# PSUM as seven single banks, maxima and exponentials in halves, and a layer schedule with its own start for each part of a visit

## The reference

```python
out = jnp.einsum('nec,ecd->nd', cb, exp_out)      # each token: the gated answers of its two experts
...
for i in range(NL):                                # NL = 6 layers
    q, k = _rope(q.reshape(B, L, H, HD)), _rope(k.reshape(B, L, H, HD))
    x = x + _attn(q, k, v, src_mask).reshape(B, L, D) @ so_w[i].T
    ...                                            # cross-attention, then the feed-forward part
```

## Time and profile before

| What | Value |
| --- | --- |
| median of 3 runs | 2237.33 us (2235.38 to 2241.73) |
| the profiled execution | 2237.12 us |
| its span, first to last instruction | 2235.3 us |
| mean granted TensorE clock | 0.905 of 2.4 GHz |
| busy, share of the span | PE 80%, PEld 34%, DVE 74%, ACT 66%, POOL 46% |
| instructions | 36409 |
| HBM traffic | 82.15 MB read, 67.85 MB written |

### The profile page before, as it was taken

The page is one execution under the profiler, slowest core; times in us unless marked ns, Lnnn a source line. Parts: engine busy times, 40 slices in busy tenths (PEclk is TensorE's granted clock), DMA queues, the critical chain, the costliest instruction groups (busy, mean ns, idle before and its releaser), DMA issues.

```text
span 2235.3 us, 36409 instructions
## 1 busy us (share of the span) xinstructions
PE 1791.6 (80%) x13134; PEld 765.2 (34%) x13138; DVE 1653.7 (74%) x3177; ACT 1476.8 (66%) x1840; POOL 1021.2 (46%) x1498
## 2 busy tenths in 40 slices
PE   3564184158899999999999999999999999998561
PEld 2332173012233333333333333333333333333331
DVE  7766111367788888888888888888888888877675
ACT  2443021026688788888888888888888888878452
POOL 2443703422345545455645445544544554534531
PEclk9766597569899999999999999999999999999765
DMA  3001121222443343334343235333244334331100
GB/s 100 1 0 38 56 85 52 67 67 37 92 96 85 66 88 79 79 87 92 83 97 78 54 84 108 95 72 87 53 103 95 82 69 94 81 78 41 30 11 10
DMA packets 153714, 154.87 MB, mean 69 GB/s; under 512 B 32247, under 2 KB 137523, under 8 KB 153523
## 3 DMA queue, kind: packets, MB, share of 16 engines
q1 hardware_dynamic: 151487, 148.34, 28.7%
q0 software_dynamic: 2048, 4.20, 0.7%
HBM read 82.15 MB, written 67.85 MB: 67 GB/s over the span
## 4 chain that ended last, share of the span: by engine, by line
PE 39%; DVE 11%; DMA 9%; ACT 7%; POOL 7%; issue 6%; SPq 2%; DVEq 0%; POOLq 0%; ACTq 0%
PE ps L1323 9%; DMA q<-scratch_queries 9%; PE ps L1287 5%; PE ps L1436 5%; PE ps L1276 4%; DVE smax L1819 4%; ACT big L1549 4%; POOL hat L126 3%; PE ps L1427 3%; PE ps L1335 2%; PE ps L1400 2%; PE ps L1310 2%; PE ps L1298 1%; DVE maxima L1826 1%; PE ps L1376 1%
## 5 line engine op out<-in xcount | busy, mean ns | idle before, releaser
L1549 ACT ACTIVATE big<-ps 128x1024 f32<-128x1024 f32 x960 | 951.9, 1023 | 241.4 <-PE ps L1287 222.3
L1819 DVE TENSOR_REDUCE smax<-ps 128x2 f32<-128x1024 f32 x768 | 921.5, 1219 | 204.4 <-PE ps L1276 181.2
L1323 PE MATMUL ps<-big,vaug 128*32 128x512 f32 x3072 | 419.8, 617 | 0.0
L1276 PE MATMUL ps<-k,q 49*128 49x512 bf16 x1536 | 298.1, 391 | 68.3 <-DMA q<-scratch_queries 51.5
L1287 PE MATMUL ps<-q,k 52*128 52x512 bf16 x1536 | 300.6, 390 | 16.1 <-DVE smax L1819 8.3
L1826 DVE TENSOR_REDUCE maxima<-ps 128x8 f32<-128x616 f32 x192 | 150.1, 795 | 42.8 <-PE ps L1310 40.5
L1276 PEld LDWEIGHTS ps<-k,q 49*128 49x128 bf16 x1536 | 72.8, 94 | 297.6 <-ACT big L1549 99.3
L1718 POOL TENSOR_SCALAR var_next<-mv_next 128x4 f32<-128x4 f32 x24 | 5.6, 233 | 356.1 <-DVE mv_next L1886 356.1
L1287 PEld LDWEIGHTS ps<-q,k 52*128 52x128 bf16 x1536 | 75.7, 94 | 187.2 <-DVE smax L1819 63.9
L1736 POOL TENSOR_TENSOR rot<-rot,cs 128x512 f32<-128x512 f32 x72 | 91.9, 1277 | 101.0 <-DVE rot L1837 101.0
L1436 PE MATMUL ps<-w,hT 128*128 128x128 f32 x768 | 112.4, 292 | 4.2 <-ACT hT L1622 4.2
(11 more groups left out here) (308 smaller groups left out, 2934.5 us busy)
## 6 DMA issues: line engine op xcount, KB each, us to landing
k<-scratch_keys SPq DMA_DIRECT2D x48, 384.0 KB
q<-scratch_queries SPq DMA_DIRECT2D x48, 384.0 KB, 8.1
cq<-scratch_cross_queries SPq DMA_DIRECT2D x48, 384.0 KB, 5.8
scratch_keys<-rparts SPq DMA_DIRECT2D x24, 384.0 KB, 2.5
scratch_queries<-rparts SPq DMA_DIRECT2D x24, 384.0 KB, 2.4
scratch_cross_queries<-rparts SPq DMA_DIRECT2D x24, 384.0 KB
scratch_keys<-rparts SPq DMA_DIRECT2D x24, 256.0 KB, 2.2
scratch_queries<-rparts SPq DMA_DIRECT2D x24, 256.0 KB, 2.7
```

The costliest lines, as they stand in the source:

```text
L1276: last = nc.tensor.matmul(out[:, u], m.q6[rows, v % 2, 2 * g + pr, qt * P:(qt + 1) * P], m.k6[rows, v % 2, 2 * g + pr, :], start=True, sto ...
L1323: last = nc.tensor.matmul(m.ps[32 * j:32 * j + 32, pv_bank, :], of_head(m.vaug, v % 2 * TB + kt, g, j), of_quad("self", q)[:, j, :], start ...
L1549: nc.scalar.activation(of_quad(kind, p // 2)[:, p % 2 * 2:p % 2 * 2 + 2, :], banks("exp" if kind == "self" else "cross exp", p), ACT.Exp, ...
L1819: nc.vector.tensor_reduce(m.smax[:, n % 2, qt, :, pr], banks("max", i), AX.X, ALU.max).then_inc(s_read["self"], 1)
```

## The change

- **Banks.** Banks 0 to 6 are seven single banks for all uses; the weighed values collect in bank 7. `shared` hands them out one at a time; a pair of scores takes two of them, wherever they lie. `bank_freed` names each use's reader. `free_pair` waits for both banks before the first of the two matmuls. `take_aux` goes.
- **Halves.** A maximum, a cross maximum, an exponential and the copies of turned rows in the closing block become two instructions, one per bank, each with an increment of its semaphore (the copies with one for both). Counts that wait for them double.
- **Fetch.** The 32 gathers and the combination move from `mixture` into `layers`, batch by batch. `begin_layers` goes: a batch's statistics run on VectorE, its root on POOL and its normalisation on VectorE, and each batch's first statistics wait for `begun`. `m.fetch` moves to the part of `big` that the third and fourth buffer of exponentials use, whose first uses wait for `begun`.
- **Places.** All tables are new. A call's place is its offset plus the start of its part in that visit, `STARTS`, with six parts per visit (`PARTS`) and 24 starts per part, instead of one period.
- The rows for the closing block's second half count on a semaphore of their own, and its bias waits for the first half's rows.

On POOL the places give the order: fetch 0, fetch 1, root 0, fetch 2, normalisation of visit 0, fetch 3, rotations of visit 0, root 1, the rest of visit 0's splitting, root 2, normalisation of visit 1, root 3, rotations of visit 1. On VectorE: combine 0, state 0, combine 1, statistics of visit 0, one rotation, combine 2, the other rotation, combine 3, state 1, statistics of visit 1, states 2 and 3, rotations of visit 1, then the first maximum. On TensorE the values of visit 0 and the turn and products of visit 1 stand before the first scores of visit 0.

```diff
@@ mixture, POOL @@
-            for u in range(2):
-                pool.wait_ge(stored[u], 16 * (EXPERTS // 2))
-            for t in range(T):
-                for k in range(TOP_K):
-                    nc.gpsimd.indirect_dma_start(m.fetch[:, k, t, :], None, a["answers"],
-                                                 bass.IndirectOffsetOnAxis(ap=m.fetch_from[:, k, t:t + 1], axis=0)).then_inc(fetched[t // TB], 16)
...
@@ Places @@
-    def put(self, name, count, first, offsets, period):
-        self.of[name] = {i: period * (i // len(offsets)) + offsets[i % len(offsets)] for i in range(first, count)}
+    def put(self, name, count, first, offsets, starts):
+        self.of[name] = {i: starts[i // len(offsets)] + offsets[i % len(offsets)] for i in range(first, count)}
...
@@ layers @@
-    pv_bank, aux = 6, 7
+    banks, pv_bank = 7, 7
...
+    def each(kind, taken, given, count, parts=2, every=1):
+        return [(at(taken, every * i), at(given, i) + u / 8, (kind, i, u)) for i in range(count) for u in range(parts)]
+    uses = each("exp", "PE exp", "ACT exp", VISITS * PER_VISIT) + each("max", "PE max", "DVE max", VISITS * PER_VISIT)
...
+    place, bank_before = shared(uses, banks)
...
+            def free_bank(kind, i, u=0):
+                if bank_before[kind, i, u] is not None:
+                    before, n, half = bank_before[kind, i, u]
+                    freed, per = bank_freed[before]
+                    pe.wait_ge(freed, n + 1 if per == 1 else 2 * n + half + 1)
+                return bank(kind, i, u)
+            def free_pair(kind, i):
+                return [free_bank(kind, i, u) for u in range(2)]
...
@@ max_scores, TensorE (shifted_scores and cross_scores alike) @@
-                out = free_banks("max", i)
+                out = free_pair("max", i)
...
@@ exponentials, ScalarE @@
-                nc.scalar.activation(of_quad(kind, p // 2)[:, p % 2 * 2:p % 2 * 2 + 2, :], banks("exp" if kind == "self" else "cross exp", p),
-                                     ACT.Exp, scale=scale).then_inc(probs[kind], 1)
+                if p % 2 == 0 and before is None and quad[kind, p // 2] >= 2:
+                    act.wait_ge(begun, B // 2 * (quad[kind, p // 2] - 1))
+                for u in range(2):
+                    nc.scalar.activation(of_quad(kind, p // 2)[:, p % 2 * 2 + u, :], bank("exp" if kind == "self" else "cross exp", p, u),
+                                         ACT.Exp, scale=scale).then_inc(probs[kind], 1)
...
@@ POOL @@
+            def fetch_answers(b):
+                for u in range(2 if b == 0 else 0):
+                    pool.wait_ge(stored[u], 16 * (EXPERTS // 2))
+                for t in range(TB):
+                    for k in range(TOP_K):
+                        nc.gpsimd.indirect_dma_start(m.fetch[:, b, k, t, :], None, a["answers"], bass.IndirectOffsetOnAxis(
+                            ap=m.fetch_from[:, k, b * TB + t:b * TB + t + 1], axis=0)).then_inc(fetched[b], 16)
...
@@ row_maxima, VectorE (cross_row_maxima alike) @@
-                nc.vector.tensor_reduce(m.smax[:, n % 2, qt, :, pr], banks("max", i), AX.X, ALU.max).then_inc(s_read["self"], 1)
+                for u in range(2):
+                    nc.vector.tensor_reduce(m.smax[:, n % 2, qt, u, pr:pr + 1], bank("max", i, u), AX.X, ALU.max).then_inc(s_read["self"], 1)
...
@@ VectorE @@
+            def combine(b):
+                dve.wait_ge(fetched[b], 16 * TOP_K * TB)
...
+                for t in range(b * TB, (b + 1) * TB):
+                    last = nc.vector.bn_stats(m.st.bn[:, t, :], m.x[:, t, :])
+                c_chain.link(last)
+                for t in range(b * TB, (b + 1) * TB):
+                    last = nc.vector.bn_aggr(m.st.mv[:, t, :], m.st.bn[:, t, :])
+                last.then_inc(begin_moments, 1)
+            def first_state(b):
+                dve.wait_ge(begin_root, b + 1)
+                for t in range(b * TB, (b + 1) * TB):
+                    last = normalise(nc.vector, m.state[:], m.x[:], t, m.st)
+                last.then_inc(begun, 1)
```

601 lines of the change are left out of this document (328 added, 273 removed), and 12 rows, old and new, of the table OFFSETS.

## The result

The changed kernel takes **2221.04 us** (median of 5 runs, 2213.04 to 2225.59) against 2237.33: 0.992 of the time before, interval [0.9892, 0.9947]. It is faster by 16 us where 70 were forecast, and inside the range.

The account below looks back on a forecast made before the run. TensorE was the near bound, busy 63.4 of 66.35 us per visit, trading banks with VectorE and ScalarE. 2237.1 - 21.8 (fetch) - 10 (placing) - 38 (banks) = 2167 us, range 2112 to 2228.

Parts of the forecast that it names:

- The step that failed: Steady visits: TensorE's wait for the load of the queries, 1.0 us per visit, was taken as unchanged.
- Banks: Steady visits: seven single banks remove half of 3.8 us of waits, 1.9 us per visit, 38 us over 20 periods.
- Halves: Split readers in each visit: VectorE +2.4 us to 58.8, ScalarE +4.0 us to 59.7, both under TensorE's 63.4.
- Waits in TensorE's queue: 72 more waits per visit, two per pair of scores, costed at 0 because running matmuls cover them; 3.7 us uncovered.
- Head and ramp: Before the steady visits: fetch inside the layers gains 21.8 us, parts placed one by one in visits 1 to 3 gain 10.
- Tail: Last visit and closing block: split copies cost about 1 us, new order unpriced; taken as 0, between -8 and +8 us.
- A: Steady visits: slower readers replace banks as what TensorE waits for; period stays 66.35 us, total 2205 us; chance 0.22.
- B: Steady visits: all waits for banks go, 76 us, total 2129 us; chance 0.10.
- C: Steady visits: halves don't overlap, ScalarE reaches 65.7 us, period 68.6, total 2250 us, slower; chance 0.11.
- D: Whole kernel: the head's gain and the halves' cost cancel, total about 2237 us; chance 0.07.
- my list of what would show the forecast wrong: ScalarE halves 0.57 us apart, period 66 us or more, first scores after 445, or tail over 8 us longer.
- the weight loads' waits for the two readers: Steady visits: score weight loads' waits for exponentials and maxima were to fall well under 78 and 63 us.

Follow-up runs that it names:

- run 5: Changed kernel with the keys' preparation put ahead of the queries' on ScalarE, POOL and SP, TensorE's and VectorE's orders kept; 2147.79 us, 0.9603.
- run 15: Changed kernel with the loads of keys and queries each cut into two halves of four head pairs, mask rows at their old place; 2140.31 us, 0.9542.
- run 7: Kernel before the change, with key and query loads cut into two halves and mask rows loaded early; 2201.68 us, 0.9834.
- run 4: Changed kernel with key and query loads cut into two halves and mask rows loaded early; 2144.09 us, 0.9562.
- run 8: Changed kernel with halved loads and early mask rows, but a pair's banks given back only after both halves are read; 2243.84 us, 1.0023.
- run 1: Kernel before the change, with only maxima, cross maxima and exponentials split into two instructions each; 2263.57 us, 1.0101.
- run 11: Changed kernel with all four batches' gathers, combinations, roots and states put first again; 2233.41 us, 0.9973.
- run 12: Changed kernel with the preparation of visits 0 to 3 placed at the later visits' distance from the maxima; 2258.72 us, 1.0082.
- run 2: Changed kernel with the two mask-row loads moved from ahead of the queries' load to after the first keys' store; 2221.61 us, 0.9913.
- run 3: Changed kernel with the two mask-row loads cut into four at the same place ahead of the queries' load; 2215.83 us, 0.9896.

## Why the prediction was wrong

**The step that failed** is the sentence "Another 1.0 us per visit is the load of the queries ..., which the change leaves". It became 2.6 us, and brought the falls of the clock with it. The change had new places for every call, and I followed them through POOL's queue in the head, but not through the preparation of a steady visit, where the keys' last part had moved behind a split of maxima on POOL and behind three stores on SP. That made 14.7 us into 18.3; with the keys first on all three queues it is 15.6 and the wait is all but gone (run 5). I had also taken the wait as a fixed cost of a transfer, while it is what is left of a chain after TensorE's work beside it. The trace of before had a sign of this, in its chain of waits over the whole span, by lines (share of the span):

```profile
PE ps L1323 9%; DMA q<-scratch_queries 9%; PE ps L1287 5%; PE ps L1436 5%; PE ps L1276 4%; DVE smax L1819 4%; ACT big L1549 4%; POOL hat L126 3%; PE ps L1427 3%; PE ps L1335 2%; PE ps L1400 2%; PE ps L1310 2%; PE ps L1298 1%; DVE maxima L1826 1%; PE ps L1376 1%
```

The landing of this load is the second of all lines there; in run 15 it is not among the first fifteen.

The steady period by its parts, before to after: wait for queries +1.5, other idle time of TensorE -1.1, busy time +0.6, in which 2.15 us more per visit ran at 1.2 GHz; together +1.07. 64.45 was forecast, with 1.0 of the wait still in it. Without the wait (run 15) the period is 63.95, so the other terms of the visits came to 0.5 us less gain than forecast.

**Banks**, -1.9 us per visit: near in size, 1.4 to 1.7 (run 7 against 15 and 4), but not for the reason given, so that the size was luck. I let half of the waits go; really the early release of a half, which I had as one point among three, carries 4.4 us per visit (run 8), and the rest of the change in the visits costs 2.7 (run 8 against 7).

**Halves**: VectorE +2.4 us per visit forecast, +2.2 measured; ScalarE +4.0, and +2.2 measured in run 1. ScalarE's exponentials start 0.50 us apart or less, not 0.52. By the table in the Trainium skill (VectorE: DVE Perf Modes, section on the TRN2 errata) they would have cost 5.0 and 5.7, as an estimate; both measured costs are less than half of it. What stands beside the table, that one large tile pays the extra time once and many small ones pay it each, holds in its direction in run 1 (0.68 us per visit lost). It is outweighed where the first half's bank is what another engine waits for (4.4 us, run 8); the Trainium skill's Perfetto Trace Analysis, Optimizing Scalar/DVE Operations, has that case: breaking up instructions may help where the reader is not saturated but holds others up.

**Waits in TensorE's queue**, 72 more per visit, costed at 0: borne out as far as runs show. In run 15 TensorE stands 1.0 us per visit in all, where 3.7 was the price without cover; no run takes the waits alone.

**Head and ramp**, 31.8: 31.5. The chain of the head held to 2.3 us. The split into 21.8 and 10 is not confirmed, as the two depend on each other (runs 11 and 12). That the sum fits to 0.3 us is in part luck: the stretch to visit 3 also holds what halves and early release do in the first visits, 9.7 us lost by halves in run 1 and 6.3 lost without early release (run 8 against 4), which the forecast counts from visit 3 on.

**Tail**, 0 within 8: 12.5 gained. The halves alone gain nothing there (run 1, 266.2 us). Without early release it is 260.4 instead of 254.2 (run 8 against 4), so about half of the gain hangs on that; the rest stays open, as the tail's new order was not run by itself.

**Rivals.** A had the right shape, waits that change their owner with the period no shorter, and 2205 us, but named the readers; the owner is a load. B did not come in the changed kernel; with the loads in halves the time comes near it, 2140 against 2129. C did not come: halves overlap. D named the right sort of outcome, a gain in the head against a loss in the visits, but not the cause. Of my list of what would show the forecast wrong, the period of 66 us or more came; the tail left its bounds on the other side. One sign was badly chosen: the weight loads' waits for the two readers. In run 15 (list of waits, 607.5 to 1822.5 us) they are

```profile
PEld ps L1315 <- DVE smax L1883: 110.8, 153, 0.9
...
PEld ps L1315 <- ACT big L1591: 29.8, 51, 1.0
```

and so together as long as before (141 and 142 us), though the period is 2.4 us shorter and TensorE stands for 1.0. At least 120 of these 141 us lie behind running matmuls, as TensorE's idle time in that stretch is 19.2 us in all. So the list of weight loads does not tell what a visit waits for.

## What to carry to other kernels

A new order is to be read queue by queue along each chain that ends in a wait, above all one through a store and a load: each call that now stands ahead on any of the queues is a term. A wait that is small today is the rest of a long chain minus the work that covers it; taking other waits away, or moving one cast, brings it out. Where several transfers must land before work can start, split them by what the first piece of work needs: that took 81 us here (run 15), and an earlier issue of the last one nothing.

## What was unexpected of the hardware

- Waits of TensorE of 2.2 to 3.8 us, one per visit of 67 us, were followed in 13 of 19 visits by a fall to 1.2 GHz of 3.4 us (once 6.8); two waits of 2.7 us had none. Before, two waits of 1.7 and 1.9 us had one, and in runs 4, 5 and 15 there was none in the steady visits. The period fell by 3.3 us in run 5 where TensorE's idle time fell by 2.3; the rest is the 1.07 us of busy time.
- Two loads of 768 KB through SP let the scores start 11.4 to 11.6 us after the first was issued, whether the second followed 1 us earlier or later (runs 2 and 3) or as in the changed kernel.
- Splitting a read of two banks of PSUM, mostly of 1024 columns, cost 0.055 us per pair on either engine (2.2 / 40, run 1).
